# The 64 indirect sends of tokens to the experts' slots stand in the last attention instead of at the start of the last feed-forward

## The reference, cut to what matters

```python
# L3 attention: a forward and a backward state-space scan over each sequence
def step(h, inp):
    dA_t, dBu_t, C_t = inp
    h = dA_t * h + dBu_t
    return (h, jnp.einsum('bdn,bn->bd', h, C_t))
# L3 feed-forward: router over E = 16 experts, K = 2 a token, capacity 1.25 * tokens * K / E = 640 slots,
# every expert _mlp(h, wg, wu, wd) = silu(h @ wg) * (h @ wu) @ wd with F = 176; a shared expert for all tokens
```

## Time and profile before

| | us |
|---|---|
| median of 3 runs | 3704.25 (3703.48 to 3706.73) |
| profiled execution, its own time | 3681.64 |
| its span in the trace | 3679.9 |
| last attention, first scan to last product | 2572.2 to 3425 |
| shared expert on TensorE | 3431.4 to 3475.6 |
| the 16 experts on TensorE | 3520.6 to 3636.8 |

### The profile page before, as it was taken

The page is one execution under the profiler, slowest core; times in us unless marked ns, Lnnn a source line. Parts: engine busy times, 40 slices in busy tenths (PEclk is TensorE's granted clock), DMA queues, the critical chain, the costliest instruction groups (busy, mean ns, idle before and its releaser), DMA issues. The chain is left out here.

```text
span 3679.9 us, 70058 instructions
## 1 busy us (share of the span) xinstructions
PE 3315.5 (90%) x24448; PEld 2238.3 (61%) x24448; DVE 2418.6 (66%) x5383; ACT 1883.3 (51%) x5083; POOL 1724.8 (47%) x1885
## 2 busy tenths in 40 slices
PE   5899997869999989999998899997999999999676
PEld 2666653647777756666665344444777777777465
DVE  3899852556666646666664344447899999999325
ACT  4777665466666635555555000006767766776123
POOL 2566531337777743333331000002677767777564
PEclk8999998989999999999999899997999999999887
DMA  4888840030000000000001686762553222223423
GB/s 125 229 222 232 227 115 11 1 78 1 2 2 1 2 1 2 2 2 1 2 2 47 143 154 150 152 138 65 120 127 98 79 83 82 82 75 88 130 85 111
DMA packets 314342, 300.54 MB, mean 82 GB/s; under 512 B 74441, under 2 KB 229513, under 8 KB 313738
## 3 DMA queue, kind: packets, MB, share of 16 engines
q1 hardware_dynamic: 309386, 286.58, 31.6%
q0 software_dynamic: 4608, 9.48, 0.8%
HBM read 237.45 MB, written 58.53 MB: 80 GB/s over the span
## 5 line engine op out<-in xcount | busy, mean ns | idle before, releaser
L2417 DVE TENSOR_TENSOR_SCAN a_h<-a_dA,a_dBu_psum 128x512 f32<-128x512 f32 x512 | 594.4, 1201 | 44.4 <-PE a_dBu_psum L1999 35.4
L2302 POOL TENSOR_TENSOR a_h<-a_h,main_g 128x512 f32<-128x512 f32 x256 | 388.4, 1522 | 170.0 <-DVE a_h L2417 168.7
L1247 POOL TENSOR_SCALAR a_probs<-a_probs,a_row_inv 128x128 f32<-128x128 f32 (+1 forms) x512 | 380.0, 763 | 163.0 <-DVE a_row_inv L1210 163.0
L1714 DVE SCALAR_TENSOR_TENSOR m_hidden<-m_h_psum,m_gate_spread 128x512 f32<-128x512 f32 x256 | 176.7, 691 | 263.2 <-PE m_h_psum L1652 250.7
L179 POOL TENSOR_TENSOR main_g<-main_g,main_s 128x512 f32<-128x512 f32 x28 | 44.1, 1607 | 647.9 <-ACT main_g L161 647.9
L1516 POOL TENSOR_TENSOR r_position_q<-r_turned_q 128x512 f32<-128x512 f32 x128 | 159.8, 1270 | 342.8 <-DVE r_turned_q L1561 342.8
L1567 DVE TENSOR_REDUCE r_neg_max<-r_logits_psum 128x2 f32<-128x512 f32 x256 | 169.9, 685 | 215.2 <-PE r_logits_psum L1383 215.2
L1472 ACT ACTIVATE r_probs<-r_logits_psum,r_neg_max 128x256 f32<-128x256 f32 x512 | 235.4, 474 | 139.9 <-DVE r_neg_max L1567 139.9
L1999 PE MATMUL a_dBu_psum<-a_B_diag,a_dt_u_turned 64*128 64x128 f32 x4096 | 298.9, 286 | 7.7 <-DVE a_h L2417 7.0
L1152 ACT ACTIVATE a_probs<-a_logits,a_neg_max 128x128 f32<-128x128 f32 (+1 forms) x512 | 226.7, 446 | 127.0 <-DVE a_neg_max L1196 127.0
L2022 PE MATMUL a_y_psum<-main_ident,a_h 128*128 128x128 f32 x2048 | 277.2, 276 | 13.6 <-POOL a_h L2302 12.3
(11 more groups left out here) (516 smaller groups left out, 7551.5 us busy)
## 6 DMA issues: line engine op xcount, KB each, us to landing
m_gate_spread<-m_gate_rows SPq DMA_DIRECT2D x64, 1024.0 KB, 8.2
main_g<-a_b_c_rows SPq DMA_DIRECT2D x256, 256.0 KB, 3.3
a_band_rows<-main_g SPq DMA_DIRECT2D x64, 512.0 KB, 4.2
a_B<-a_band_rows SPq DMA_DIRECT2D x192, 128.0 KB, 3.4
a_A<-a_band_rows SPq DMA_DIRECT2D x192, 128.0 KB, 3.2
f_x_expert<-f_x_rows SPq DMA_DIRECT2D x16, 322.5 KB, 2.8
f_x_rows<-a_zero SPq DMA_DIRECT2D x16, 320.0 KB, 5.0
f_stage_w<-L_ffn_up_weights SPq DMA_DIRECT2D x9, 512.0 KB, 7.2
```

The costliest lines, as they stand in the source:

```text
L1247: ins = nc.gpsimd.tensor_scalar(pr[:, h % NPR, tile[t]], pr[:, h % NPR, tile[t]], rinv[:, p % NST, q:q + 1], None, ALU.mult)
L2302: tt(h[:, at, :, :], h[:, at, :, :], Cs[:, r % NCS, :, :], ALU.mult).then_inc(hc_pool, 1)
L2417: nc.vector.tensor_tensor_scan(flat, dA[:, M % NDA, q, k, :, :].rearrange("p n t -> p (n t)"), db[:, 2 * (g % 2) + q, :], 0.0, ALU.mult, A ...
```

## The change

The sends move into the attention. They stand in units 3 to 15, at steps `j` of 3, 5, 7, 8 and 9, five a unit, the last four in unit 15. They are issued from a ring of four tiles `rows_out`: six steps ahead of a tile's first send SyncE fetches its tokens from `f_x_tokens` (`fill`, one DMA of 128 KB for both choices) and ScalarE writes the numbers (`name_rows`, 128x2 elements). VectorE makes `row_ids` once, in `place`. The clears stand every second step instead of every fourth, so that they end at step 38, before unit 3. In the feed-forward `iota`, VectorE's copy, the 16 loads `take_tokens` and the waits for the sends are gone; SyncE waits for them at the end of the attention instead.

```diff
+        NR, SENDS, FIRST_SEND = route.NR, (3, 5, 7, 8, 9), 3
+        rows_out = s.sb("rows_out", [P, NR, TOPK, P + 1])
...
+        def sends(g):
+            U, j = g // STEPS, g % STEPS
+            if U < FIRST_SEND or j not in SENDS:
+                return None
+            n = len(SENDS) * (U - FIRST_SEND) + SENDS.index(j)
+            return (n // TOPK, n % TOPK) if n < NT * TOPK else None
+
+        FILL = 6
...
+                def name_rows(n):
+                    if n == 0:
+                        act.wait_ge(indexed, 1)
+                    if n >= NR:
+                        act.wait_ge(sent[n % NR], 16 * TOPK * (n // NR))
+                    ac(rows_out[:, n % NR, :, P], row_ids[:, n, :], ACT.Copy).then_inc(ring_id, 1)
...
+                    if sends(g + FILL) and sends(g + FILL)[1] == 0:
+                        name_rows(sends(g + FILL)[0])
...
+                def fill(n):
+                    sp.wait_ge((tokens_lo, tokens_hi)[n // 16], 16)
+                    if n >= NR:
+                        sp.wait_ge(sent[n % NR], 16 * TOPK * (n // NR))
+                    src = route.x_tok[n].rearrange("p (o f) -> p o f", o=1).broadcast_to([P, TOPK, P])
+                    sp.dma_start(rows_out[:, n % NR, :, 0:P], src).then_inc(ring_in[n % NR], 16)
...
-                    if g >= FIRST_CLEAR and g % 4 == 0 and (g - FIRST_CLEAR) // 4 < E:
-                        clear((g - FIRST_CLEAR) // 4)
+                    if g >= FIRST_CLEAR and g % 2 == 0 and (g - FIRST_CLEAR) // 2 < E:
+                        clear((g - FIRST_CLEAR) // 2)
+                    if sends(g + FILL) and sends(g + FILL)[1] == 0:
+                        fill(sends(g + FILL)[0])
...
-                sp.wait_ge(cleared, 16 * 3 * E)
+                for i in range(NR):
+                    sp.wait_ge(sent[i], 16 * TOPK * len(range(i, NT, NR)))
...
+                def send(n, k):
+                    if n == 0 and k == 0:
+                        pool.wait_ge(indexed, 1)
+                        pool.wait_ge(cleared, 16 * 3 * E)
+                    if k == 0:
+                        pool.wait_ge(ring_in[n % NR], 16 * (n // NR + 1))
+                        pool.wait_ge(ring_id, n + 1)
+                    nc.gpsimd.indirect_dma_start(route.x_rows, bass.IndirectOffsetOnAxis(ap=route.dest_u[:, n, k:k + 1], axis=0),
+                                                 rows_out[:, n % NR, k, :], None).then_inc(sent[n % NR], 16)
...
                         if j == 10:
                             times_u(U + 1, 0)
                             times_u(U + 1, 1)
+                    if sends(g):
+                        send(*sends(g))
...
+                    ts(row_ids[:], spare_row[:], -float(E * CAP), None, ALU.add)
...
-                nc.gpsimd.iota(ids[:], pattern=[[P * TOPK, NT], [1, TOPK]], base=0, channel_multiplier=TOPK).then_inc(id_made, 1)
-                pool.wait_ge(id_sb, 1)
-                for n in range(NT):
-                    pool.wait_ge(rows_in[n // 4], 16 * TOPK)
-                    if n >= NSENT:
-                        pool.wait_ge(sent[n % NSENT], 16 * TOPK * (n // NSENT))
-                    for k in range(TOPK):
-                        nc.gpsimd.indirect_dma_start(route.x_rows,
...
-                take_tokens(0)
                 for dst, src in ((wg[:, E, :], d["sw_gate"]), (wu[:, E, :], d["sw_up"]),
                                  (wd[:, E], d["sw_down"].rearrange("(a p) n -> p a n", p=FH))):
                     sp.dma_start(dst, src).then_inc(shared_in, 16)
-                for m in range(1, QUADS):
-                    take_tokens(m)
...
-                for i in range(NSENT):
-                    sp.wait_ge(sent[i], 16 * TOPK * len(range(i, NT, NSENT)))
                 for e in range(E):
                     ask_rows(e)
```

More of the change, by code:

```diff
@@ L1874, in l3_attention @@
         c_rd = [s.sems(f"c_rd{i}") for i in range(NCS)]
+        ring_in = [s.sems(f"ring_in{i}") for i in range(NR)]
+        sent = route.sent
+        ring_id = s.sems("ring_id")
+        def sends(g):
[5 more added lines that the diff above has]
+        FILL = 6
         (u_mm, z_mm, low_mm, b_mm, dt_mm, dtuT_mm, dbu_mm, y_mm, yzd_mm, out_mm, tx_sb, u_act, z_raw, z_sb, low_sb, b_sb,
@@ L2460, with __init__ @@
 class Route:
-    def __init__(self, nc, s, tokens):
+    def __init__(self, nc, s, tokens, sent):
         self.E, self.TOPK = 16, 2
@@ L2467, in __init__ @@
         self.NT, self.PER = tokens // P, self.CAP // P
+        self.sent, self.NR = sent, len(sent)
         assert self.CAP == self.PER * P and self.NT * self.E == BANK
@@ L2477, in slots, with last_layer @@
         return rows[e * self.CAP:(e + 1) * self.CAP, :].rearrange("(p t) f -> p t f", t=self.PER)
-def last_layer(nc, c, d_attn, d_ffn, x, xn, s, g):
+def last_layer(nc, c, d_attn, d_ffn, sent, x, xn, s, g):
     with Scope(nc, "l4") as q:
-        route = Route(nc, q, xn.shape[1])
+        route = Route(nc, q, xn.shape[1], sent)
         l3_attention(nc, c, d_attn, d_ffn, route, x, xn, s, g)
@@ L2502, in l3_ffn @@
         sg, hm = s.sb("silu", [FH, NH, 2, T]), s.sb("hidden", [FH, NH, 2, T])
-        two = s.sb("two_rows", [P, NT, TOPK, P + 1])
-        ids = s.sb("ids", [P, NT, TOPK], mybir.dt.int32)
+        two = s.sb("two_rows", [P, NT, TOPK, P])
         acc = s.sb("acc", [P, NG, P])
         tr, gp, upp, op = s.banks("turned", 2), s.banks("gate", 2), s.banks("up", 2), s.banks("o", 2)
-        (turn_mm, turn_sb, g_mm, u_mm, silued, hidden, o_mm, o_sb, weighed, combined, back_mm, added, id_made, id_sb, goal_sb, x_in,
+        (turn_mm, turn_sb, g_mm, u_mm, silued, hidden, o_mm, o_sb, weighed, combined, back_mm, added, goal_sb, x_in,
          shared_in, loaded) = s.sems(
-            "turn_mm turn_sb g_mm u_mm silued hidden o_mm o_sb weighed combined back_mm added id_made id_sb goal_sb x_in "
+            "turn_mm turn_sb g_mm u_mm silued hidden o_mm o_sb weighed combined back_mm added goal_sb x_in "
             "shared_in loaded")
-        rows_in = [s.sems(f"rows_in{m}") for m in range(QUADS)]
         y_in = [s.sems(f"y_in{m}") for m in range(QUADS)]
-        sent = [s.sems(f"sent{i}") for i in range(NSENT)]
         y_out = [s.sems(f"y_out{i}") for i in range(NX)]
@@ L2706, in _ @@
             def _(sp):
-                def take_tokens(m):
-                    for k in range(TOPK):
-                        sp.dma_start(two[:, 4 * m:4 * m + 4, k, 0:P],
-                                     route.x_tok[4 * m:4 * m + 4].rearrange("n p f -> p n f")).then_inc(rows_in[m], 16)
                 def ask_rows(e):
@@ L3593, in build @@
         c = make_constants(nc, m)
+        sent = m.sems("sent0 sent1 sent2 sent3")
         with Scope(nc, "f0") as f:
@@ L3599, in build @@
         third_layer(nc, c, part("L2_attn"), part("L2_ffn"), x, xn, s, g)
-        last_layer(nc, c, part("L3_attn"), part("L3_ffn"), x, xn, s, g)
+        last_layer(nc, c, part("L3_attn"), part("L3_ffn"), sent, x, xn, s, g)
         gate_and_norm(nc, c, x, xn, s, g, gate=True, norm=False, out=out)
```

7 lines of the change are left out of this document (2 added, 5 removed).

## The result

The change made the kernel slower: 3753.65 us (median of 4 runs, 3748.16 to 3756.73) against 3704.47 before on the same chip, a ratio of 1.013 (95% interval 1.0113 to 1.0148). That is 49 us more where 32 less were predicted. The profiled execution took 3748.16 us, with a span of 3746.4.

The account below looks back on a forecast made before the run. TensorE was taken to bound the attention, GpSimd's 64 sends the feed-forward's front. 3681.64 - 47.4 + 15.1 + 0.1 = 3649.4 us profiled, 32.2 less; from the median 3704.25 that gives 3672.0 us, range 3656 to 3688.

Parts of the forecast that it names:

- The gap: Between shared expert and expert 0, TensorE waits for the slots' read behind 64 sends; 44.98 us would go.
- the start: TensorE's shared expert starts sooner, its weights no longer queued behind two token loads: 0.97 us gained.
- the restart: Expert 0's first matmuls no longer run at the low clock that follows the gap: 1.5 us gained.
- The cover: Fills, numbers, denser clears, C's rows and feed-forward weights arrive in time, hidden behind other work.
- Step 9's send: Behind add_log, ahead of times_u: all 1.26 us reach TensorE in units 3 to 14, 15.1 us; bounds 10 to 22.
- Steps 3, 5, 7 and 8 ... Cost 0: Sends ahead of add_log: GpSimd 0.56 us late, caught by its 4.21 us of idle; cost 0.
- Rival C: Earlier sends cost too: GpSimd's spread holds VectorE's product 0.79 us, 1.2 us a unit; 3687.5 us, chance 0.16.
- Rival E: Every send in the attention delays TensorE by its full length, 64 x 1.26 = 80.6 us; 3737 us, chance 0.04.
- Rival D: Sends in the attention are held behind VectorE's scans, 12 x (1.26 + 2.3) = 43 us; 3700 us, chance 0.05.
- B: Step 9's send hides as well, TensorE catching up its 1.26 us before the next logarithm; 3657 us, chance 0.10.
- F: Expert 0 waits for weights or slots and half of the 45 us gap stays; 3695 us, chance 0.03.
- The 22.6 us that no row explained: The profiled execution of the kernel before lay 22.6 us below the runs' median, 3704.25; the difference was taken over.

Follow-up runs that it names:

- the moved sends: Changed kernel with sends at steps 2, 4, 6, 8 and 9, directly behind `times_c`, where GpSimd waits next: 3633.9 against 3680.37 us for the kernel before, 0.9872.
- the stand-in: Kernel before, with a GpSimd tensor_tensor of 128x384 at the 64 places of the new sends, its own sends left in the feed-forward: 3688.86 against 3680.37 us, 1.002.
- one send of five moved: Changed kernel with only step 9's send moved ahead of `add_log`, the others kept: 3762.92 against 3707.51 us for the kernel before, 1.0148.
- three in a row: Changed kernel with sends at steps 4 and 6 and three behind product 9, ahead of `add_log`: 3648.88 against 3707.51 us for the kernel before, 0.9846.
- the dense clears: Kernel before with only the clears twice as dense, every second step instead of every fourth: 3708.52 against 3707.51 us, 1.0.

## Why the prediction was wrong, point by point

- **The gap, 44.98 us, the start, 0.97, and the restart, 1.5**: the mechanism is right, and so is the sum of 47.4 for a chip like that of the profile: the kernel without sends in the attention and the one with well placed sends are 50 and 46 us faster than before on theirs. From the last scan to the first matmul of the shared expert it is 15.0 us in place of 16.3, 1.2 sooner, near the 0.97. The 16 experts take 114.4 us with the moved sends and 116.5 with the stand-in, which has the restart, on one chip: 2.1 us for the 1.5. But the sum was taken from a profile of the one kind of chip and set against a median of the other; on the chip of the result these terms gave about 60 us (last section).
- **The cover**: right. Weights, fills, numbers, clears and C's rows cost nothing that can be measured (1.0 for the clears; 46 us gained with all of them in place). A send takes 1.02 us (median) and lands in 2.8 us.
- **Step 9's send, 12 x 1.26 = 15.1 us**: the mechanism exists, its size was too large. The arithmetic stand-in of 1.27 us shows 8.5 us, some 0.7 a unit. In the changed kernel it can't be told from what follows. GpSimd's idle time before `add_log`, forecast to fall from 4.21 to 3.6 us, fell to 0.27 (3.06 with the sends moved).
- **"Steps 3, 5, 7 and 8 ... Cost 0" is the step that failed**, with the bounds of step 9's term. I counted only GpSimd's lateness and found idle time to absorb it. GpSimd's time was indeed not short: with the sends moved, the kernel is 46 us faster with all 64 in the attention. The cost fell on VectorE. Sends at 5 and 7 stand ahead of a spread and a product that are ready, and VectorE asks 0.87 us into them: 3.07 and 3.06 us in place of 0.67. Step 9's holds the product for 6.01. Per unit that is 10.1 us more, less what the 1.45 and the 1.08 us products of before had already lost (1.2, of which 0.4 stay): 9.3 us. The unit grew by 8.35, the rest went into VectorE's own idle time. For twelve units this is 100 us, and unit 15, with three products held, brings the attention to 109 us. Less the 60 us that the feed-forward gives on such a chip, this is the loss of 49.
- **Rival C named the place** (VectorE's product held) **and mis-sized it**: I priced a hold by the longest row of before, 1.45 us, as if VectorE always got in at the next boundary, 1.2 us a unit in its sum. No row of before had a send next to work on VectorE that mattered, and that was where the bound should have been wide. **Rival E** had the right sign and the wrong cause. **Rival D** had the wrong direction: it is VectorE that waits. Behind scans no send was held (1.02 us, the first of all 1.21, as in the kernel before); only the 13 sends of the changed kernel that start while VectorE's product still runs, for another 0.39 us, are longer, 1.29 us (the row at 3003.84), 0.27 us and not 2.3. B and F are out.
- **The Trainium skill**, "SBUF — State Buffer", section "SBUF: two separate sides", says that a VectorE instruction with two SBUF inputs and a GpSimd instruction that reads SBUF exclude each other, the first one for its whole instruction. The runs agree with the exclusion, and with "the whole instruction" where no send is near (1.35 us). After a send they differ: the product stays out over six further GpSimd instructions (7.93 us). What it says on sends that starve behind a VectorE instruction in a two-port mode is not tested: no run here shows a send beside an instruction known to be in one.
- **The 22.6 us that no row explained** lie in the feed-forward, and most likely differ by chip; see the last section.

## What to carry to other kernels

An indirect DMA issued from GpSimd is short, but what stands directly behind it on GpSimd decides its price. If that work is ready, VectorE's instructions with two SBUF inputs may be shut out until GpSimd next stands idle. Put the send where GpSimd must wait next, or make a gap behind the first instruction after it by a wait on its own semaphore. A place is right only as long as GpSimd still waits there: with one send of five moved, the gap was gone. When an edit puts a kind of instruction beside work beside which no row shows it, price the neighbour's instructions too, not only the slack of the engine that issues it.

## What the runs showed of the hardware that was not expected

**The held run.** Without a send VectorE's product entered at GpSimd's next instruction boundary (1.35, 1.46, 1.08 us); with a send at the head of the run it stayed out for 3.07, 6.01 and 7.93 us. A stop of 0.09 us ended it, ahead of the request or behind it. Every such stop is also a wait for a semaphore, and the two weren't separated. Why a send changes this isn't settled; the runs show only what starts the state and what ends it.

**Where no stop shows.** One request a unit doesn't fit the rule as it stands, that of the product asked for in the spread directly behind the send of step 3. Two such products of the changed kernel, and GpSimd's run around the first:

```profile
2986.00 0.86 DVE L2472 TENSOR_TENSOR a_h<-a_h,main_g 128x512 f32<-128x512 f32 x1
...
3231.47 2.20 DVE L2472 TENSOR_TENSOR a_h<-a_h,main_g 128x512 f32<-128x512 f32 x1
...
2984.16 1.02 POOL L2357 DMA_INDIRECT f_x_rows<-a_rows_out,l_dest  x1 [0.16 <-issue]
2985.21 1.10 POOL L2327 TENSOR_SCALAR_AFFINE_SELECT a_B_diag<-a_B_turned 128x1024 f32<-128x1024 f32 x1
2986.27 1.72 POOL L2336 TENSOR_TENSOR a_h<-a_h,main_g 128x512 f32<-128x512 f32 x1
```

The first is asked for 0.31 us before the spread ends and gets in right there, although GpSimd's next instruction shows no gap; so it goes in ten of the twelve units 3 to 14. In unit 11 (3231.47) it is asked for 0.41 us before the spread's end, in unit 3 0.71 us, and there it stays out to the end of the run, 2.20 and 2.50 us. GpSimd's product behind this spread needs the same scans as VectorE's, and elsewhere it starts 0.23 us after VectorE's (3012.24 and 3012.01 in the kernel before). By this estimate it was free only 0.08 us before the spread ended in the ten units, and 0.18 us or more in the two. It looks as if a next instruction that comes free so late counts as a stop. That is a reading of twelve requests; no run tests it.

**Two chips' feed-forward.** The chip with the median of 3680.37 us and those with 3704 to 3707 differ behind the attention. Timeline rows of the kernel with the dense clears, whose feed-forward is that of before, on a chip of the second kind (the shared expert's first matmul, a wait of VectorE and ScalarE each, expert 0's start and the last expert's end):

```profile
3435.04 2.01 PE L2556 MATMUL f_gate_psum<-main_xn,f_w_gate 128*88 128x256 f32 x4 [7.55 <-DMA f_w_down<-L_ffn_sw_down]
...
3515.65 0.69 DVE L2660 TENSOR_TENSOR f_hidden<-f_up_psum,f_silu 88x512 f32<-88x512 f32 x1 [22.03 <-remote]
...
3504.39 0.59 ACT L2618 ACTIVATE f_silu<-f_gate_psum 88x512 f32<-88x512 f32 x1 [26.05 <-DMA f_x_tokens<-a_h]
...
3538.18 0.60 PE L2537 MATMUL f_turned_psum<-main_ident,f_x_expert 128*128 128x128 f32 x4
...
3663.66 1.50 PE L2572 MATMUL f_o_psum<-f_w_down,f_hidden 88*128 88x128 f32 x12
```

While the sends run, ScalarE stands for 26.05 and VectorE for 22.03 us. Not all of it is a wait for inputs: TensorE had ended the gate matmuls that ScalarE reads at 3488.64, 15.7 us before ScalarE starts, and VectorE's last input was there at 3504.98, 10.7 us before it starts. The releaser named for ScalarE is a transfer long done. From the shared expert's first matmul to expert 0 it is 103.1 us (3538.18 - 3435.04), against 89.2 in the profiled execution of before. From expert 0's start to the end of the last expert's product it is 127.0 us, against 116.2 in the profiled execution of before (which ends at 3636.76); the changed kernel has 127.3 (3702.95 - 3575.68), the stand-in's, on the chip of 3680.37, has 116.5. These two differences, 14 and 11 us, answer to the 22.6 us by which that execution lay below the median, which the prediction could not explain: it looks like one of the first kind. It also means that on such a chip the change gains more in the feed-forward: the changed kernel goes from the shared expert to expert 0 in 43.5 us (3575.68 - 3532.16), 59.6 less than the 103.1 of the dense clears. In the same way the moved sends gain 58.6 us with three in a row there, against 46 on the other. What ScalarE and VectorE wait for isn't shown by any row and wasn't tested, and the two best versions weren't timed on one chip, so they are not ranked.
